# Fourth graph layer: gather plain node rows and apply two basis matrices per node, instead of gathering from a table of eight relations

## The reference, cut to what matters

```python
def _L3_gnn_ref(feat, W, coeff, h_bias, loop_weight, src, dst, etypes):
    msg = coeff[etypes][:, :, None] * feat[src][:, None, :]      # 2 bases x 64 per edge
    agg = jax.ops.segment_sum(msg, dst, num_segments=n_nodes)    # node x 2 x 64
    h = agg.reshape(n_nodes, num_bases * in_feat) @ W.reshape(num_bases * in_feat, out_feat)
    h = h + h_bias
    h = h + feat @ loop_weight
    return h
x = _layernorm(x + _L3_gnn_ref(x, W, coeff, h_bias, loop_weight, src, dst, edge_type_8), axis=-1)
```

## Time and profile before

| | us |
|---|---|
| median of 3 runs (lowest, highest) | 5208.63 (5200.48, 5215.69) |
| the profiled execution | 5216.39 |
| its span, first to last instruction | 5214.5 |

### The profile page before, as it was taken

How to read it: one execution, slowest core, us unless ns; L and a number is a source line. 1 busy time by engine, 2 the same in 40 slices (tenths; PEclk the granted TensorE clock), 3 DMA queues, 4 the chain that set the end, 5 groups by cost and what they waited for, 6 DMA issues and landing times. The chain is left out here.

```text
span 5214.5 us, 29259 instructions
## 1 busy us (share of the span) xinstructions
PE 1381.8 (26%) x5965; PEld 649.7 (12%) x5965; DVE 2573.3 (49%) x6949; ACT 1058.4 (20%) x3112; POOL 3722.9 (71%) x3641
## 2 busy tenths in 40 slices
PE   7000000000000000000577788888847200000000
PEld 3000000000000000000233333333315100000000
DVE  4444433334355555555358777887768222222223
ACT  2000000000000000000257677777744100000000
POOL 0777777776777777776777777777723577777776
PEclk9555555555555555555789898898868655555555
DMA  6222222221122322222135545545433211111111
GB/s 239 73 73 73 72 73 73 73 74 55 48 84 76 84 76 83 76 79 60 52 102 187 197 168 197 192 173 196 170 146 117 73 50 54 50 54 50 54 50 45
DMA packets 186876, 511.78 MB, mean 98 GB/s; under 512 B 69783, under 2 KB 72986, under 8 KB 176824
## 3 DMA queue, kind: packets, MB, share of 16 engines
q1 hardware_dynamic: 68824, 381.39, 19.5%
q0 software_dynamic: 117856, 128.36, 10.8%
HBM read 183.80 MB, written 325.51 MB: 98 GB/s over the span
## 5 line engine op out<-in xcount | busy, mean ns | idle before, releaser
L178 POOL DMA_INDIRECT AR<-xt,Si x1664 | 1746.0, 1049 | 507.2 <-issue 501.4
L454 DVE SCALAR_TENSOR_TENSOR AR<-AR,gf 128x64 f32<-128x64 f32 x1662 | 475.1, 286 | 1486.9 <-DMA AR<-y,I 785.9
L178 POOL DMA_INDIRECT AR<-y,R x832 | 857.2, 1030 | 367.4 <-issue 238.3
L178 POOL DMA_INDIRECT AR<-y,I x832 | 788.4, 948 | 336.2 <-issue 238.6
L996 PE MATMUL ps<-AR,WLR 128*128 128x512 f32 x1248 | 668.4, 664 | 0.0
L1152 DVE SCALAR_TENSOR_TENSOR AR<-AR,gf 128x390 f32<-128x390 f32 x780 | 485.5, 622 | 174.8 <-ACT AR L1138 153.3
L1138 ACT ACTIVATE AR<-AR 128x64 f32<-128x64 f32 x1664 | 501.6, 353 | 0.0
L1003 ACT ACTIVATE AR<-ps 128x512 f32<-128x512 f32 x624 | 374.9, 601 | 131.4 <-PE ps L996 129.1
L352 PE MATMUL ps<-AR 128*98 128x64 bf16 x832 | 80.1, 271 | 1021.0 <-DVE AR L346 1021.0
L797 PE MATMUL ps<-AR,ones 128*128 128x384 f32 (+1 forms) x6 | 3.7, 757 | 1231.0 <-DVE AR L758 1231.0
L650 DVE TENSOR_TENSOR AR<-AR 128x1024 f32<-128x1024 f32 x52 | 64.8, 1246 | 443.5 <-DMA AR<-xt,Si 443.5
(11 more groups left out here) (268 smaller groups left out, 2398.4 us busy)
## 6 DMA issues: line engine op xcount, KB each, us to landing
s<-AR SPq DMA_DIRECT2D x52, 3168.0 KB
s<-AR SPq DMA_DIRECT2D x104, 512.0 KB, 2.7
AR<-xd SPq DMA_DIRECT2D x104, 512.0 KB
s<-AR SPq DMA_DIRECT2D x52, 528.0 KB, 3.2
xd<-AR SPq DMA_DIRECT2D x52, 512.0 KB, 3.7
AR<-xt,Si POOLq DMA_INDIRECT x1664
y<-AR SPq DMA_DIRECT2D x24, 1024.0 KB, 3.9
AR<-y,R POOLq DMA_INDIRECT x832
```

Of the source, the lines that this page charges most:

```text
L178: g.indirect_dma_start(out=o, out_offset=None, in_=table, in_offset=bass.IndirectOffsetOnAxis(ap=idx, axis=0)).then_inc(S[sem], 16)
L454: v.scalar_tensor_tensor(out=buf[:, j, :], in0=buf[:, j - 1, :] if j else prev[:, CH - 1, :], scalar=gf[:, c * CH + j:c * CH + j + 1], in1 ...
```

## The change

The table of relations is gone. X is stored once to a DRAM table `xt3` of 64-wide rows, and the gathers fetch by `Si`, the source node alone. DVE forms for each chunk a one-hot of the edge types, from it the two coefficients of each edge, and multiplies: each gathered row of 64 gives a row of 128 (its product with either coefficient). The running sums, their store and the nodes' fetch are then 128 wide. At the end PE transposes each node's 128-wide sum and multiplies it by the stacked bases. The self-loop product stands after the third layer's node stage, and its DVE part inside the first chunks. ACT's last loop has the copies of group q+1 ahead of the square root of group q. The core of the diff:

```diff
-    y3 = dram("y3", (NN * R3, D))
+    xt3 = dram("xt3", (NN, D))
-    s3 = dram("s3", (EP + 1, D))
+    s3 = dram("s3", (EP + 1, NBS * D))
...
+        def basis_chunk_g(e, c):
+            b = c % NBUF
+            buf = GB[:, b, :].rearrange("p (j d) -> p j d", j=CH)
+            if c >= NBUF:
+                e.wait_ge(S["m3"], 4 * (c - NBUF + 1))
+            for j in range(CH):
+                gather(buf[:, j, :], xt3, Si[:, c * CH + j:c * CH + j + 1], f"g_{b}")
+
+        def basis_chunk_v(e, c):
+            cur, prv = s3v(c), s3v(c - 1)
+            m3c.then(lambda: v.tensor_tensor(OH3, bc(E8[...].unsqueeze(2), [P, CH, R3]),
+                                             bc(lo64[:, 0:R3].unsqueeze(1), [P, CH, R3]), ALU.is_equal))
+            m3c.then(lambda: v.tensor_tensor(PR3..., bc(OH3.unsqueeze(1), [P, NBS, CH, R3]),
+                                             bc(cov.unsqueeze(2), [P, NBS, CH, R3]), ALU.mult))
+            m3c.then(lambda: v.reduce_sum(CW3, PR3.rearrange("p b (j r) -> p b j r", r=R3), AX))
+            e.wait_ge(S[f"g_{b}"], gathered_before(3, b) + 16 * CH * (c // NBUF + 1))
+            if c >= 3:
+                e.wait_ge(S[f"s_{c % 3}"], stored_before(3, c % 3) + 16 * (c // 3))
+            m3c.then(lambda: v.tensor_tensor(S3[:, c % 3, :].rearrange("p (j b d) -> p j b d", j=CH, b=NBS),
+                                             bc(buf.unsqueeze(2), [P, CH, NBS, D]),
+                                             bc(CW3.rearrange("p b j -> p j b").unsqueeze(3), [P, CH, NBS, D]), ALU.mult))
+            for j in range(CH):
+                v.scalar_tensor_tensor(out=cur[:, j, :], in0=cur[:, j - 1, :] if j else prv[:, CH - 1, :],
+                                       scalar=gf[:, c * CH + j:c * CH + j + 1], in1=cur[:, j, :], ...)
...
-        def table3_t(e, q): ...
-        def table3_a(e, q, i): ...
-        def table3_y(e, q, i): ...
+        def loop3_t(e, q): ...        # the self-loop products alone
...
+        def bases_t(e, q):
+            for l in range(GN):
+                m = t.transpose(PS[l // 4][...], NG3[:, q % 2, l * P:(l + 1) * P], ident[:])
+            e.wait_ge(S["ata"], 2 * (q + 1))
+            for l in range(GN):
+                m = t.matmul(PS[5 + q % 2][:, l * D:(l + 1) * D], AT3[:, q % 2, l * P:(l + 1) * P], WB[:], start=True, stop=True)
+        def bases_a(e, q): ...        # two copies, PS to AT3
         def nodes3_v(e, q):
-            c.then(lambda: v.tensor_tensor(nb, nb, R[:, sl, :], ALU.add))
+            c.then(lambda: v.tensor_tensor(nb, ps, R[:, sl, :], ALU.add))
...
-            for r in range(R3):                # DVE, first layer: building W3
-                vc.then(lambda: v.tensor_scalar(W3[:, r * D:(r + 1) * D], wb[:, 0, :], ...))
-                vc.then(lambda: v.scalar_tensor_tensor(out=W3[...], in0=wb[:, 1, :], ...))
...
+                e.wait_ge(S["kn"], q + 1)      # SP, once per node group
+                load(e, rows_view(xt3, sl), X[:, sl, :].rearrange("p l d -> p (l d)"), "xt")
...
             for q in range(NG):                # ACT, at the end
+                if q + 1 < NG:
+                    bases_a(e, q + 1)
                 e.wait_ge(S["n3"], K3 * q + 7)
                 s.sqrt(rs, rs).then_inc(S["na"], 1)
```

More of the change, by code:

```diff
@@ L17 @@
 R3 = 8
+NBS = 2
 H = 6
@@ L59, in stored_before @@
 def stored_before(L, b):
-    return sum(16 * len(range(b, NCH, n)) for n in (4, 3, 2, 4)[0:L] if b < n)
+    return sum(16 * len(range(b, NCH, n)) for n in (4, 3, 2, 3)[0:L] if b < n)
 def bc(a, shape):
@@ L467, in stored_all, with mend_linear_g, mend_linear_t, mend_linear_v @@
                 e.wait_ge(S[f"s_{b}"], stored_before(L, b) + 16 * len(range(b, NCH, n)))
-        def mend_linear_g(e, L, st):
-            stored_all(e, L, NBUF)
-            gather(fr0, st[:], fixg[:], "rowg")
+        def mend_linear_g(e, L, st, w, nbuf):
+            stored_all(e, L, nbuf)
+            gather(fr0[:, 0:w], st[:], fixg[:], "rowg")
             e.wait_ge(S["fr"], 1 * (L + 1))
-            scatter(st[:], fr0, fixs[:], "rows")
-        def mend_linear_t(e, L):
+            scatter(st[:], fr0[:, 0:w], fixs[:], "rows")
+        def mend_linear_t(e, L, Tl, w):
             e.wait_ge(S[f"lin{L}"], NC - 1)
-            t.matmul(PS[2][:, 0:D], Cq[:], Tl0, start=True, stop=True).then_inc(S["pmd"], 1)
-        def mend_linear_v(e, L):
+            t.matmul(PS[2][:, 0:w], Cq[:], Tl, start=True, stop=True).then_inc(S["pmd"], 1)
+        def mend_linear_v(e, L, w):
             e.wait_ge(S["rowg"], 16 * (L + 1))
             e.wait_ge(S["pmd"], 1 + L // 3)
-            v.tensor_tensor(fr0, fr0, PS[2][:, 0:D], ALU.add).then_inc(S["fr"], 1)
+            v.tensor_tensor(fr0[:, 0:w], fr0[:, 0:w], PS[2][:, 0:w], ALU.add).then_inc(S["fr"], 1)
         def node_gathers(L, q, NBt, st):
@@ L1370, in table3_t @@
             for l, w, i in pairs_of(q * GN, GN):
-                xt_ = xtt[0:w * D, q % 2, i * P:(i + 1) * P]
                 for hf in range(w):
[L1373 to L1390, removed]
-                s.copy(ysb3[:, k % 4, hf * RT3:hf * RT3 + 512], PS[5 + y % 2][:]).then_inc(S["pya"], 1)
-        def table3_y(e, q, i):
-            l, w, k = q * GN + 2 * i, 2 if i < 3 else 1, 4 * q + i
-            e.wait_ge(S["pya"], 7 * q + 2 * i + w)
-            load(e, y3v[:, l * RT3:(l + w) * RT3], ysb3[:, k % 4, 0:w * RT3], f"ys{k % 4}")
+                    m = t.matmul(PS[(4, 7)[hf]][:, i * D:(i + 1) * D], xtl[0:w * D, q % 2, i * P:(i + 1) * P],
+                                 LW[0:w * D, hf, :], start=True, stop=True)
+            m.then_inc(S["lp"], 1)
         def loop3_v(e, q):
@@ L1769, in _ @@
             e.wait_ge(S["fr"], 3)
-            for hf in range(2):
-                tuc.up(v.memset(W3z[(1 - hf) * D:(2 - hf) * D, hf, :], 0.0))
-                tuc.up(v.tensor_copy(W3z[hf * D:hf * D + D, hf, :], W3[hf * D:hf * D + D, :]))
             weighted_v(e, 0)
@@ L1844, in _ @@
             projected_t(e, 0)
-            for q in range(NG + 1):
-                if q:
-                    table3_t(e, q - 1)
-                if q + 1 < NG:
-                    projected_t(e, q + 1)
-                if q < NG:
-                    turn3_t(e, q)
-            mend_linear_t(e, 3)
+            for q in range(1, NG):
+                projected_t(e, q)
+            e.wait_ge(S["kn"], NG)
+            for q in range(NG):
+                turn3_t(e, q)
+                loop3_t(e, q)
+            mend_linear_t(e, 3, Tl3, NBS * D)
+            for q in range(NG):
+                bases_t(e, q)
 _INS = ["x", "src", "dst", "edge_type_16", "edge_type_8", "L0_gnn_weight", "L1_gnn_beta", "L2_gnn_W_l", "L2_gnn_W_r",
```

141 lines of the change are left out of this document (87 added, 54 removed), and 4 rows, old and new, of the table names.

## The result

| | before | after |
|---|---|---|
| median on the same chip, us | 5210.47 (5200.48 to 5215.69, 4 runs) | 5304.22 (5301.12 to 5318.18, 4 runs) |
| profiled execution, us | 5216.39 | 5305.03 |
| its span, us | 5214.5 | 5303.2 |

The ratio is 1.0187, with a 95% interval from 1.0164 to 1.0211: the change makes the kernel 1.9% slower. The forecast was 5300.

A forecast was written before the change was run, and what follows sets the result against it. POOL's gather issue rate was taken as the bound, 20.0 us a chunk. Terms -23 + 99.6 + 7.1 + 7.3 = +91 us on the profiled 5216.4 gave 5307, median 5300; range 5236 to 5328.

The forecast's parts named there:

- Rule of rows 3 and 4: Gathers beginning during a two-SBUF-input DVE product stand until its end, finishing 0.82 us after; DVE 0.03 us ahead lets them through.
- the rival on the other side: Fourth-layer gathers: DVE's product does not hold POOL because both inputs are broadcast views; -16 us, 5193; chance 0.06.
- (a): Fourth-layer gathers: still 832 rows 64 wide, POOL's own work stays 20.0 us a chunk, nothing gained by the smaller table.
- (b): Product of 128 x 2048 per chunk: 2.29 us long, stops gathers; 46 x 2.06 + 5 x 0.96 = 99.6 us.
- (c): Running-sum steps of 128 and coefficient work: 352 ns steps, DVE hidden under POOL, gathers stretched 7 us, bounds 5 and 18.
- (d): Chunk store of 1024 KB instead of 512: 3.9 us to land instead of 2.7, hidden by three buffers except the last.
- (e): Node stage before the gathers, without table work: POOL starts 23 us earlier, bounds 16 and 33.
- (f): Tail after the gathers: last product, wider steps, store, PE transposes and products, less fetch savings; +7.3 us, bounds +4 and +10.
- (g): Kernel start: 16 DVE steps building W3 go, a memset and an SP wait come, ahead of DVE's 5.33 us wait; 0.
- Mostly through: Fourth-layer product starts late enough to let the gather through in most chunks; +40 us, 5249; chance 0.22 with mixtures.
- The product doesn't hold POOL: Fourth-layer gathers unheld since both product inputs are broadcast views; -16 us, 5193; chance 0.06.
- The clock gives all back: PE's clock in the node stage returns the relation-work saving, wide steps hit every gather; +117 us, 5326; forecast's upper end.

The follow-up runs named there:

- run 2: Kernel before plus an unread DVE reduction of 128 x 2048, one SBUF input, per fourth-layer chunk; 5845.19 us, ratio 1.0001 to the kernel before on its chip.
- run 7: Changed kernel with each row's two coefficients in PSUM instead of SBUF; 5895.99 us, ratio 1.0070 to the kernel before on its own chip.
- run 5: Changed kernel with the chunk's product cut into 16 DVE pieces of 128; 5837.75 us, ratio 1.0067, and again 5848.67 us, ratio 1.0077.
- run 1: Kernel before plus an unread DVE product of 128 x 2048 behind each fourth-layer chunk's landing; 5860.29 us, ratio 1.0041 to the kernel before on its chip.
- run 3: Changed kernel with a small DVE memset ahead of each chunk's product, so it starts later; 5896.16 us, ratio 1.0079 to the kernel before on its chip.
- before_plus_reduce: Kernel before plus an unread DVE reduction of 128 x 2048 per fourth-layer chunk, in place of a test product; 5845.19 us, ratio 1.0001.
- coef_psum: Changed kernel with one edit, the coefficients CW3 in PSUM instead of SBUF; 5895.99 us, ratio 1.0070 to the kernel before on its own chip.
- coef_psum_filler: Changed kernel with coefficients in PSUM and four idle TensorE matmuls ahead of each last-node-stage group but the first; 5882.18 us, ratio 1.0042.

## Why the prediction was right, by its own steps

**Rule of rows 3 and 4.** It held: held gathers end 0.82 us after the product, and the edge lies near 0.05 us. The tests add that it needs both inputs in SBUF (runs 2 and 7) and that it is not one product but an unbroken run of small ones that can count (run 5). The doubt over broadcast views, the rival on the other side, is gone: the probe of run 1 has two of them and holds the gather.

The Trainium skill, "SBUF — State Buffer", section "Who interferes with whom", says that a VectorE instruction with at most one SBUF input, outside the modes that use two ports, does not contend with GpSimd. The runs agree, with 0.94 us under the reduction (run 2) and under the product with its coefficients in PSUM (run 7). Its account of a probe in which a tensor_tensor stalled no DMA descriptors is not borne out: 3.03 us in run 1.

**(a)** Gathers that met nothing kept 0.94 us, and POOL its 0.30 of issue. **(b)** 99.6 us forecast. The product measured 2295 ns against 2.29 us. 47 gathers were stopped at once and 4 got through, for 46 and 5: the offsets of the kernel before were the right ones to take, and the second wait did not move them. The 51 held gathers cost 100.7 us. **(c)** Steps of 128 took 355 ns against 352. The rest of the gathers' growth, over the 3.8 us that the kernel before has, is 7.1 us, as forecast. (b) and (c) together came to 107.8 us against 106.7, and POOL never waited for DVE. This cover is worth naming: where DVE's instructions come 1.40 us apart, as in the experiments, 20 of them outlast the 20 us of gathers, and (c) is not hidden.

**(d)** The store stayed hidden, but for the last. **(e)** The first gather began at 4054.41 against 4058. The row in front of it and those of the last two finishings in the changed kernel's timeline:

```profile
3962.66 0.62 DVE L1315 TENSOR_TENSOR AR<-ps,b 128x448 f32<-128x448 f32 x1 [3.02 <-PE ps L1295]
3981.34 0.62 DVE L1315 TENSOR_TENSOR AR<-ps,b 128x448 f32<-128x448 f32 x1
...
4035.60 9.22 PE L1295 MATMUL ps<-W,AR 128*128 128x64 f32 x42 [0.63 <-ACT AR L1305]
4044.86 0.62 DVE L1315 TENSOR_TENSOR AR<-ps,b 128x448 f32<-128x448 f32 x1 [12.65 <-PE ps L1295]
4051.58 0.62 DVE L1335 TENSOR_TENSOR X<-AR 128x448 f32<-128x448 f32 x1
4054.41 0.94 POOL L179 DMA_INDIRECT AR<-xt,Si  x1 [65.59 <-DMA xt<-X]
```

DVE waits 3.02 us for PE in one group and not at all in the next: the groups stand 18.7, 21.8, 18.7, 21.8, 21.7 and 20.0 us apart, as the products of each are at the full clock (4.90 us) or the low one (9.22). My 23 us lay between the bounds of 16 and 33 for the same mixture, guessed in its share and not derived: that it was met closely is luck. Of the 26.45 us, 3.11 arose before this stage (its first product began at 3897.47 and not at 3900.58), which no step of mine had. That too is chance: over the three layers before, the same POOL instruction starts anywhere from 6.7 us later to 3.3 us earlier in the changed kernel's trace, back and forth, as now one kernel's gather meets a DVE instruction and now the other's (1.39 us and 0.94 at the same place). The stage itself gave 23.34. X complete to the first gather took 2.2 us against 2.7.

**(f)** The total of 7.3 us was right, its terms were not. The last group in the changed kernel's timeline:

```profile
5290.45 1.75 PE L1449 MATMUL ps<-ident,AR 128*128 128x128 f32 x7 [3.85 <-DMA AR<-s,endi]
5291.66 1.06 ACT L1464 COPY AR<-ps 128x512 f32<-128x512 f32 x2 [8.25 <-PE ps L1449]
5292.77 3.25 PE L1456 MATMUL ps<-WB,AR 128*128 128x64 f32 x14 [0.57 <-ACT AR L1464]
5296.06 0.62 DVE L1472 TENSOR_TENSOR AR<-ps,R 128x448 f32<-128x448 f32 x1 [2.34 <-PE ps L1456]
```

The mis-sized term is the seven products: 3.25 us, not 7 x 0.22 = 1.54. The count on the row is 14, not 7: each fp32 product of this form is two records, and the x42 of rows 7 are 21 products. I had divided 9.22 us by 42 and counted one record for each product. PE's leg from the landing to DVE is 5.6 us and not 4.0. On the other side the 49 fetches have a mean of 990 ns against 1043 in rows 10: 2.6 us and not 1.5. The mend's fetch comes 14.13 us after the last gather, against 10.30 in the kernel before: 3.8 us for the product, the wider steps and the store, not 3.4 + 1.2. That makes 5.6 - 2.6 + 3.8 = 6.8 of the 7.3. The rest lies in POOL's two waits in the mend (4.29 and 1.53 us, against 4.07 and 1.44) and in the way from the last fetch's end to the engine that takes it up (1.59 against 1.44). So the total was met by luck: I had PE's leg 1.6 us too short, and against it the fetches 1.1 us and the product, steps and store 0.8 us too long. The square root's new place behind the copies did not move the end.

**(g)** Not separated; nothing in the comparison speaks of it.

**The rivals.** "Mostly through" (5249) fell with 4 of 51 through; run 3, which made it come about, shows that it would have cost 1.0 to 1.2 us a chunk, as its term of 0.96 had it. "The product doesn't hold POOL" (5193) fell in the result and in run 1; run 7 shows what it takes to make it true. "The clock gives all back" (5326) was half true of the mechanism, and its price stayed within its bound.

## What to carry to other kernels

Where POOL's indirect DMAs set the pace, "DVE is idle there anyway" is not a licence: ask of each DVE instruction beside them whether both its inputs are in SBUF, and price it at what is left of it when the next gather begins. If it must be there, put the small operand into PSUM, which removed the hold without a further instruction (that it shortens the whole kernel is an estimate for a chip like the first, and was not seen on the others); of the cuts, halves brought the stretch from 76 to 38 us, sixteen pieces only to 62. Work that is hidden with 10 of 20 us to spare on one chip was not hidden on another: count its instructions as well as its busy time, and count a matmul's records before dividing by them.

## What the runs showed of the hardware that I had not expected

- A run of 16 two-input DVE instructions of 0.3 us, back to back, can make a gather last 2.73 us, to 0.82 us after the last (run 5); in chunks in which a gather begins no more than 0.04 us after the first of them, none is held (15 of 15, against 55 of 55 held in the others).
- The same program takes 5210 us on one chip and 5796 to 5857 on others. There DVE's and ACT's instructions come in long stretches 0.70 or 1.40 us apart instead of 0.39 or less, with no longer busy time of their own and for DVE and ACT alike; 17 DVE instructions to a chunk then give 23.8 us (before_plus_reduce), 20 give 28.0 (coef_psum). The stretches go with the place in the program: the 13th to 16th distances between chunks are 23.1, 24.1, 32.9 and 41.7 us in coef_psum, and 23.1, 24.1, 32.9 and 41.8 in coef_psum_filler. The even step and the like effect on both engines look like a limit on how fast instructions reach an engine, but no run tested that, and the packets of the instruction queues take no longer there (211 of 556 ns on average in coef_psum, 211 of 555 in the changed kernel on the first chip).
- Four matmuls of 128x512 took 3.65 us at the full clock and 4.65 to 6.24 where the clock rose on the way; the clock was low again by the next group's products in about every other group.
